# Attention rows with the maxima inside the query buffer, and the first expert layer joined to its normalisation

## The chip, the cores and the metric

The kernel runs on one core of a Trainium2 chip. The metric is the device time of one execution in microseconds. A profiled execution gives the trace; the other runs give times alone.

## What is computed

Two transformer layers with adaptive normalisation over 1024 tokens of width 256, in float32 with some bfloat16 in the expert part. Cut to what matters here:

```
layer 0: x -> modulated layer norm -> attention, 16 heads of 16, 1024 queries against 4096 keys
         scores = Q K^T / 4;  attn = softmax(scores);  out = attn V;  x += gate * (out Wo^T)
         x -> modulated layer norm -> router over 8 experts, top 2, softmax weights
         h = silu(x w1) * (x w3), bfloat16, 8 experts of 64 units;  x += gate * (weights, h w2)
layer 1: x -> modulated layer norm -> attention, 16 heads of 16, 1024 queries against 1024 keys, projection, bias
         x -> norms -> causal attention, 16 heads of 128 -> router over 16 experts, top 6
         -> experts of 176 units and a shared one of 352;  x += gate * result
```

## The kernel before, in words

All instructions are written out by hand for each engine, with semaphores between them; each `nc.Block()` ends in a barrier of all engines. The order within an engine is the order of the code.

**Narrow attention** (class `Attention`, `run`, used for both layers; `nkt` is 32 key tiles of 128 in layer 0 and 8 in layer 1). A unit `u` is one half (512 queries) of one head, 32 units per layer. Every unit has two passes. The *first pass* (`first_half`, L706) multiplies queries by keys so that VectorE can take the row maxima (L901 in layer 0, L896 in layer 1); a chunk is a pair of products, one on each *strip* of TensorE's rows (rows 0 to 63 and 64 to 127), which run side by side. The *second pass* (`second_chunk`, L770) computes the transposed scores minus the maximum, tile by tile on alternating strips, ScalarE takes the exponential (L1003) and the value products (`values_part`, L749) sum probabilities times values. Queries and keys are split in a high and a low part, 16 rows each, so a strip has 48 rows for the first pass and 51 for the second, the last three of which are the maximum in three parts against rows of ones in the keys. PSUM has four banks for the first pass, a ring of three (4 to 6) for the second, bank 7 for the values.

**The turn of the maxima.** The maximum of a query lies in a column; the second pass needs it as a row. GpSimd splits it in three bfloat16 parts (`split_max`, L624 to L630), written twice, for both strips, into a field of 115 columns that is zero elsewhere. `turn_maxima(u)` on TensorE (L722) first multiplies the query rows by an identity (L728, 112 rows to 115 rows, 512 columns), then adds four products that turn the parts (L733), so that one PSUM bank holds queries and maxima. ScalarE copies it to the buffer `q_max` (`put_row`, L952), which the second pass reads. The turn for unit `u + 1` stands ahead of `second_chunk(u, turn_at)`, with `turn_at = nkt - 6`, that is 26 in layer 0 and 2 in layer 1, and takes one place in the ring of three banks.

In `slot_long` (layer 0) the order on TensorE for four key tiles j to j + 3 is:

```
second(j)  first_pair(strips 1, 0)  second(j + 1)  values, half 0
second(j + 2)  second(j + 3)  first_pair(strips 0, 1)  values, half 1
```

`second(j)` is the turn if it is due, the wait for the bank (the exponential three places earlier in the ring), and the product. Even j are on strip 0, odd on strip 1. `slot_short` (layer 1) is `second(j)`, `first_pair(1, 0)`, `second(j + 1)`, the turn if due, `first_pair(0, 1)`, `second(j + 2)`, `second(j + 3)`, values.

SyncE issues nearly all transfers in one queue: it stores each unit's result (L152), loads the next head's query rows (`send_rows`, L73; three parts for each strip) into one of `nb` buffers `q_rows` (3 or 4), and its keys (L432) and values (L435). ScalarE issues six transfers at the start of layer 1 alone.

**The front** of layer 0 (`Front`, and the loop over `ahead` chunks in `run`) computes the modulation, the first norm and the query projection; `pick_queries` (L839) puts the first head's queries in place, and `half_product` (L1390) of the projection stands between the first chunks.

**After the first attention** come two blocks: `normalise` "n1" (L1284: statistics, square root on ScalarE at L1339, transposes L1332, the normalised, transposed tokens `h_t` at L1319 and L1346; SyncE loads the router's and the experts' weights in it, L1272) and `experts_low` (L1505: eight filling products, 32 router products L1584, ScalarE casts the weights at L1619 to L1624, VectorE ranks the experts L1473 to L1482 and then makes their weights L1493 to L1501; the up products L1557, SiLU L1609, `weigh` L1643 and L1647, transposes L1566, down products L1577). `experts_high` (L2225 on) uses the same `rank_experts` and `best_softmax`; there the first hidden product of VectorE (L2509) stands between the two. `keep_busy` (L1281) are products whose result nobody reads.

## Time and profile before

| | |
|---|---|
| median of 3 runs | 1763.31 us (1759.29 to 1764.13) |
| the profiled execution | 1766.98 us, its span in the trace 1765.1 us |
| TensorE busy | 1702.8 us, 96% of the span |
| VectorE, ScalarE, GpSimd busy | 1390.3, 1151.6 and 525.8 us |
| granted TensorE clock | 0.987 of full, mean |
| layer 0 attention | from about 53 to 736 us |
| norm and experts of layer 0 | 736 to 783 us |
| layer 1 narrow attention | 783 to 1024 us |
| wide attention, then the experts of layer 1 | to 1534, to the end |

A busy TensorE is not one at its peak, since ends of products are modelled; the starts are what the trace measures, so paces are read between starts. A row of the timeline merges equal instructions that follow each other: its second number is from the first one's start to the last one's end.

### The profile page before, as it was taken

What the parts mean: (1) busy time and instruction counts of PE and PEld (TensorE: products, weight loads), DVE (VectorE), ACT (ScalarE), POOL (GpSimd) and SP (SyncE); (2) the same over time, 40 slices, a digit from 0 to 9 for tenths busy, and PEclk for the clock granted to TensorE, in tenths of its full rate; (3) what the DMA queues carried; (4) which work ended last, traced back from release to release, by engine and by line L of the source; (5) the groups of instructions that cost most, each with busy time, mean ns of one, the idle gap of its engine ahead of it and who ended that gap; (6) DMA issues with size and microseconds to landing.
All of it is one profiled execution on the core that took longest, in us unless ns stands there. A gap on an engine that the chain in (4) does not pass through costs nothing. (4 is left out here: it accounts for less than half of the span.)

```text
span 1765.1 us, 33568 instructions
## 1 busy us (share of the span) xinstructions
PE 1702.8 (96%) x12503; PEld 1042.5 (59%) x12506; DVE 1390.3 (79%) x1930; ACT 1151.6 (65%) x2279; POOL 525.8 (30%) x549
## 2 busy tenths in 40 slices
PE   9999999999999999889999989999999999899998
PEld 6433333333333333565444468888888888778886
DVE  6999999999999996367999667677777777566665
ACT  3788888888888887555888545455545555543433
POOL 7646334334444512002334301110211120044221
PEclk8999999999999999989999999999999999999999
DMA  5223222223322300103546210000000000034332
GB/s 169 50 46 59 47 52 53 48 46 73 70 47 58 77 20 11 37 19 60 134 100 168 70 33 16 9 24 15 24 9 24 15 12 1 13 102 114 104 106 77
DMA packets 50329, 97.48 MB, mean 55 GB/s; under 512 B 11313, under 2 KB 21649, under 8 KB 48771
## 3 DMA queue, kind: packets, MB, share of 16 engines
q1 hardware_dynamic: 50019, 95.58, 22.5%
q8 instruction: 78, 1.28, 0.3%
q10 hardware_dynamic: 192, 0.30, 0.1%
q14 instruction: 40, 0.33, 0.1%
HBM read 64.58 MB, written 15.92 MB: 46 GB/s over the span
## 5 line engine op out<-in xcount | busy, mean ns | idle before, releaser
L1003 ACT ACTIVATE a_probs<-psum 128x512 f32<-128x512 f32 x1280 | 693.1, 597 | 122.5 <-PE psum L770 94.0
L901 DVE TENSOR_REDUCE a_max_part<-psum 128x1 f32<-128x1024 f32 x512 | 621.3, 1223 | 40.0 <-PE psum L706 37.1
L770 PE MATMUL psum<-a_q_max,a_k_rows 51*128 51x512 f32 x1280 | 409.5, 466 | 0.8 <-ACT a_probs L1003 0.7
L749 PE MATMUL psum<-a_probs,a_v_ext 128*32 128x256 f32 (+1 forms) x4600 | 395.2, 415 | 7.0 <-issue 6.9
L706 PE MATMUL psum<-a_k_rows,a_q_rows 48*128 48x512 f32 x1280 | 354.3, 428 | 1.1 <-ACT a_q_rows L969 0.7
L770 PEld LDWEIGHTS psum<-a_q_max,a_k_rows 51*128 51x128 f32 x1280 | 167.0, 184 | 270.0 <-ACT a_probs L1003 215.0
L749 PEld LDWEIGHTS psum<-a_probs,a_v_ext 128*32 128x32 f32 x4600 | 91.4, 108 | 207.1 <-ACT a_probs L1003 105.4
L706 PEld LDWEIGHTS psum<-a_k_rows,a_q_rows 48*128 48x128 f32 x1280 | 152.1, 186 | 17.0 <-DVE a_max_part L901 6.8
L896 DVE TENSOR_REDUCE a_neg_max<-psum 128x1 f32<-128x1024 f32 x128 | 150.8, 1219 | 8.4 <-PE psum L706 8.1
L2360 PE MATMUL psum<-high_t_parts,high_gu 128*128 128x512 f32 x600 | 148.0, 396 | 0.8 <-DVE high_hid L2509 0.8
L624 POOL TENSOR_TENSOR a_max_bf<-a_neg_max,a_zeros 128x8 bf16<-128x8 f32 x64 | 14.6, 228 | 431.1 <-issue 391.3
L461 POOL TENSOR_TENSOR a_k_rows<-a_k_in,a_k_rows 16x2048 fp32r<-16x2048 f32 x30 | 137.0, 4565 | 2.3
L1924 PE MATMUL psum<-wide_k_t,wide_q_t 128*128 128x512 f32 (+3 forms) x576 | 130.5, 353 | 1.5 <-DVE wide_k_t L2122 1.5
L2360 PEld LDWEIGHTS psum<-high_t_parts,high_gu 128*128 128x128 f32 x600 | 113.5, 190 | 27.9 <-POOL high_gu L2477 1.4
L1924 PE MATMUL psum<-wide_p_t,wide_v 128*128 128x512 f32 (+3 forms) x576 | 109.7, 344 | 5.1 <-DVE x L2133 5.1
L1924 PEld LDWEIGHTS psum<-wide_p_t,wide_v 128*128 128x128 f32 x576 | 97.6, 188 | 22.5 <-issue 6.3
L2065 ACT ACTIVATE wide_probs<-psum,wide_neg_max 128x128 f32<-128x128 f32 (+7 forms) x128 | 96.4, 753 | 21.6 <-DVE wide_neg_max L2155 21.6
L2144 DVE TENSOR_TENSOR wide_p_t<-psum,wide_p_t 128x512 fp32r<-128x512 f32 (+1 forms) x192 | 99.9, 548 | 12.4 <-ACT wide_p_t L2050 12.4
L1924 PE MATMUL psum<-wide_t_parts,wide_wqk 128*128 128x512 f32 x384 | 102.2, 401 | 6.1 <-DVE wide_v L2122 3.9
L2050 ACT ACTIVATE wide_p_t<-psum 128x512 fp32r<-128x512 f32 (+1 forms) x192 | 87.1, 493 | 28.1 <-PE psum L1965 28.1
L1924 PEld LDWEIGHTS psum<-wide_k_t,wide_q_t 128*128 128x128 f32 x576 | 94.0, 189 | 12.6 <-issue 1.9
L2155 DVE TENSOR_REDUCE wide_neg_max<-psum 128x1 f32<-128x128 f32 (+7 forms) x128 | 97.0, 758 | 4.4
(282 smaller groups left out, 2162.7 us busy)
## 6 DMA issues: line engine op xcount, KB each, us to landing
o<-a_o_out SPq DMA_DIRECT2D x56, 256.0 KB, 2.3
a_k_in<-in_k SPq DMA_DIRECT2D x90, 128.0 KB, 4.6
a_q_rows<-q_high SPq DMA_DIRECT2D x122, 64.0 KB, 2.4
gu_in<-in_w_gu SPq DMA_DIRECT2D x25, 256.0 KB, 2.9
high_cw<-cw SPq DMA_DIRECT2D x22, 256.0 KB, 4.0
a_v_in<-in_v SPq DMA_DIRECT2D x16, 256.0 KB, 5.8
a_o<-o SPq DMA_DIRECT2D x8, 512.0 KB, 4.2
wide_qk_in<-in_wqk SPq DMA_DIRECT2D x16, 256.0 KB, 2.7
```

The lines of the kernel that those rows point to most:

```text
L461: pool.tensor_tensor(self.k_rows[low, b, :], self.k_in[low, :], self.k_rows[low, b, :], ALU.subtract).then_inc(self.k_split, 1)
L706: return pe.matmul(psum[:, 2 * (n % 2) + s, :], q_rows[rows, b, q0:q0 + P], k_rows[rows, b, k0:k0 + 512], start=True, stop=True)
L749: mm = pe.matmul(psum[32 * g:32 * g + 32, 7, cols], self.v_ext[:, b, block_at, :], self.probs[:, j % self.pring, cols], start=(j < 4 and f ...
L770: pe.matmul(psum[:, self.bank_of(self.filling(j)), :], k_rows[rows, b, k0:k0 + P], self.q_max[rows, u % 2, :], start=True, stop=True).then ...
L896: dve.tensor_reduce(self.neg_max[:, u % 2, c:c + 1], psum[:, 2 * (n % 2):2 * (n % 2) + 2, :], AX.XY, ALU.max, negate=True).then_inc(self.s ...
L901: dve.tensor_reduce(self.max_part[:, u % 2, qt, ch:ch + 1], psum[:, 2 * (n % 2):2 * (n % 2) + 2, :], AX.XY, ALU.max).then_inc(self.s1_free, 1)
L1003: act.activation(self.probs[:, p % self.pring, :], psum[:, self.bank_of(self.filling(j)), :], ACT.Exp).then_inc(self.exp_done, 1)
L1924: mm = pe.matmul(out, left(a), right(b), start=(first and n == 0), stop=(last and n == len(PARTS) - 1))
L2065: act.activation(probs[:, i % 2, 0:(i + 1) * P], bank_pair(i)[:, 0:(i + 1) * P], ACT.Exp, bias=neg_max[:, i:i + 1], accum_out=den[:, h % 2 ...
L2144: dve.tensor_tensor(turned_of(i, bank, 1), turned_from(i, bank), turned_of(i, bank, 0), ALU.subtract).then_inc(pt_lo, 1)
L2155: dve.tensor_reduce(neg_max[:, i:i + 1], bank_pair(i)[:, 0:(i + 1) * P], AX.X, ALU.max, negate=True).then_inc(max_ready, 1)
L2360: mm = pe.matmul(psum[:, 2 * (k % 2) + i, :], gu[:, par, a, at:at + P], t_parts[:, b, c, half * 512:(half + 1) * 512], start=(c == 0 and n ...
```

## The change

The change has several parts.

1. A strip is now 64 rows for both passes: rows 0 to 15 of the keys are ones, and rows 0 to 2 of the queries hold the maximum's three parts; the query parts move to rows 16 to 63. The second pass reads `q_rows`; `q_max` and the product with the identity (L728) are gone. The turn is four products with three columns each, ScalarE copies three rows into the first strip (`put_row`), and one key tile later it issues a transfer of these rows into the second strip (`copy_row`), for which `second_chunk(u, 1)` waits (`row_copied`). When a buffer is loaded for a new head SyncE also sends zeros into the rows 0 to 2 of each strip, two transfers per head (`zero_maxima`). `turn_at` is 25 in layer 0; in layer 1 it stays 2.
2. The experts' weights of layer 0 are loaded at unit 6 of the first attention and cast by GpSimd at units 8 to 10 (class `LowWeights`). `normalise` becomes the class `Normal`, whose instructions share one block with `experts_low`; 20 and 8 filling products there are gone, and the router products begin with half of the tokens.
3. `rank_experts` computes maximum and difference ahead of the ranking instead of after it (both expert layers), and `experts_low` reorders ScalarE.
4. ScalarE loads the table of the square root at the end of both narrow attentions and of `experts_low`.
5. Fourteen filling products follow `pick_queries(0, 2)` in the front.

```
-        self.turn_at = nkt - 6
+        self.turn_at = nkt - (7 if nkt > 8 else 6)
...
+    def zero_maxima(self, sp, b):
+        sp.wait_ge(self.zeros_ready, 1)
+        zero = self.zeros[0:MROWS, 0:P].unsqueeze(1).broadcast_to([MROWS, TT, P])
+        for first in (0, STRIP):
+            sp.dma_start(self.q_rows[first:first + MROWS, b, :].bitcast(F32).rearrange("p (a n) -> p a n", n=P), zero).then_inc(self.q_loaded[b], 16)
...
                     load_q(sp, (0, 1), q_rows[:, got % nb, :], got, self.q_loaded[got % nb])
+                    if got >= nb:
+                        self.zero_maxima(sp, got % nb)
...
+                if low_weights is not None and u == 6:
+                    low_weights.load(sp, front)
+                if low_weights is not None and u == 16:
+                    low_weights.given_back(sp)
...
+                if low_weights is not None and u in (8, 9, 10):
+                    low_weights.round(pool, u - 8)
...
-                pe.matmul(psum[0:QMAX_ROWS, bank, :], self.ident_r[0:STRIP + MROW, 0:QMAX_ROWS],
-                          q_rows[0:STRIP + MROW, b, half * QH:(half + 1) * QH], start=True, stop=False)
                 pe.wait_ge(self.max_ready, u + 1)
                 for t in range(4):
-                    parts = self.max_bf[:, u % 2, t, :, :].rearrange("p s r -> p (s r)")
-                    mm = pe.matmul(psum[0:QMAX_ROWS, bank, t * P:(t + 1) * P], parts[:, 0:QMAX_ROWS], self.ident_bf[:, :], start=False, stop=(t == 3))
+                    mm = pe.matmul(psum[0:MROWS, bank, t * P:(t + 1) * P], self.max_bf[:, u % 2, t, :], self.ident_bf[:, :], start=True, stop=True)
...
                 if j == 0:
                     pe.wait_ge(self.row_ready, u + 1)
+                if j == 1:
+                    pe.wait_ge(self.row_copied, 16 * (u + 1))
...
-                          self.q_max[rows, u % 2, :], start=True, stop=True).then_inc(self.s2_full, 1)
+                          q_rows[rows, b, half * QH:(half + 1) * QH], start=True, stop=True).then_inc(self.s2_full, 1)
...
                 pick_queries(0, 2)
+                keep_busy(pe, psum, self.ident_bf, 14, 3)
...
+            def copy_row(u):
+                act.wait_ge(self.row_ready, u + 1)
+                act.dma_start(rows_of_maxima(u, STRIP).bitcast(F32), rows_of_maxima(u, 0).bitcast(F32)).then_inc(self.row_copied, 16)
...
                     if j == self.turn_at and u + 1 < us:
                         put_row(u + 1)
+                    if j == self.turn_at + 1 and u + 1 < us:
+                        copy_row(u + 1)
...
+            act.activation(self.one[:, :], self.zeros[:, 0:1], ACT.Sqrt).then_inc(self.table_loaded, 1)
...
+    def load(self, sp, front):
+        router, gate, up, down = self.drams
+        sp.wait_ge(front.later_taken, 8)
+        sp.dma_start(self.router[:, :, :], router).then_inc(self.loaded, 16)
+        sp.dma_start(self.up_in[:, 0, :, :], gate).then_inc(self.loaded, 16)
+        sp.dma_start(self.up_in[:, 1, :, :], up).then_inc(self.loaded, 16)
+        sp.dma_start(self.down_in, down).then_inc(self.loaded, 16)
+    def round(self, pool, n):
+        if n == 0:
+            pool.wait_ge(self.loaded, 64)
+        if n < 2:
+            pool.tensor_copy(self.up[:, n, :, :], self.up_in[:, n, :, :]).then_inc(self.cast, 1)
+        else:
+            pool.tensor_copy(self.down_bf[:, :, :], self.down_in).then_inc(self.cast, 1)
+            pool.wait_ge(self.cast, 3)
+            pool.tensor_copy(self.down[:, :, :], self.down_bf[:, :, :]).then_inc(self.wide, 1)
...
     step(dve.tensor_copy(s[:, :, :].rearrange("p t e -> p (t e)"), scores))
+    step(dve.tensor_reduce(best[:, :], s[:, :, :], AX.X, ALU.max))
+    dve.tensor_tensor(e[:, :, :], s[:, :, :], best[:, :].unsqueeze(2).broadcast_to([P, TT, n_exp]),
+                      ALU.subtract).then_inc(less_ready, 1)
...
-            keep_busy(pe, psum, ident_bf, 8)
             for t in range(TT):
+                if t % 4 == 0:
+                    normal.half_ready(pe, t // 4)
...
-            for i in range(2):
-                act.activation(w_bf[:, i, :, :], w_in[:, i, :, :], ACT.Copy).then_inc(w_ready, 1)
             act.wait_ge(one_set, 1)
             act.activation(one[:, 1:2], one[:, 0:1], ACT.Exp).then_inc(table_loaded, 1)
...
+            act.wait_ge(less_ready, 1)
+            act.activation(e[:, :, :], e[:, :, :], ACT.Exp).then_inc(exp_ready, 1)
             take_hidden(0)
+            silu(0)
             take_hidden(1)
-            silu(0)
             silu(1)
```

## Rows read from the trace of the kernel before

**Rows 1.** Window, length; busy PE, PEld, DVE, ACT, POOL; clock, DMA share, GB/s.

```profile
200.00:400.00 200.00, 197.52 (x1913) 75.32 (x1905) 189.50 (x166) 176.58 (x330) 74.68 (x61) 1.00 0.27 51
```

**Rows 2.** Timeline of PE around one turn, first attention: start, length, engine, line.

```profile
315.72 0.64 PE L749 MATMUL psum<-a_probs,a_v_ext 128*32 128x256 f32 x8
316.29 0.72 PE L706 MATMUL psum<-a_k_rows,a_q_rows 48*128 48x512 f32 x2
...
316.95 0.64 PE L749 MATMUL psum<-a_probs,a_v_ext 128*32 128x256 f32 x8
317.52 0.49 PE L728 MATMUL psum<-a_q_rows,a_ident_r 112*115 112x512 f32 x1
317.85 0.39 PE L733 MATMUL psum<-ident_bf,a_max_bf 128*115 128x128 bf16 x4
318.17 0.50 PE L770 MATMUL psum<-a_q_max,a_k_rows 51*128 51x512 f32 x2
```

**Rows 3.** Timeline of DVE, first attention: the end of two units' maxima.

```profile
314.63 0.17 DVE L907 TENSOR_REDUCE a_neg_max<-a_max_part 128x4 f32<-128x16 f32 x1
...
335.30 0.17 DVE L907 TENSOR_REDUCE a_neg_max<-a_max_part 128x4 f32<-128x16 f32 x1
```

**Rows 4.** Timeline of PE near the end of the first attention.

```profile
711.96 0.50 PE L770 MATMUL psum<-a_q_max,a_k_rows 51*128 51x512 f32 x1
712.39 0.70 PE L307 MATMUL psum<-a_w,h_t 128*128 128x256 f32 x2
```

**Rows 5.** DMAs of line L73, issue durations ns min/median/max, and landing of all.

```profile
L73 ACTq DMA_DIRECT2D a_q_rows<-q_high x2: 612/1048/1485, 796.1 to 797.7; - x2
...
DMA to landing us min/median/max: 1.9/2.3/7.5
```

**Rows 6.** Timeline of PE and ACT, layer 1 narrow attention.

```profile
837.30 0.49 PE L770 MATMUL psum<-a_q_max,a_k_rows 51*128 51x512 f32 x1
...
838.96 0.50 PE L770 MATMUL psum<-a_q_max,a_k_rows 51*128 51x512 f32 x2
...
842.99 0.49 PE L770 MATMUL psum<-a_q_max,a_k_rows 51*128 51x512 f32 x1
...
837.83 1.08 ACT L1003 ACTIVATE a_probs<-psum 128x512 f32<-128x512 f32 x2 [0.54 <-PE psum L770]
...
840.92 2.07 ACT L1003 ACTIVATE a_probs<-psum 128x512 f32<-128x512 f32 x4 [0.45 <-PE psum L770]
```

**Rows 7.** Timeline of all engines after the first attention.

```profile
736.19 1.28 ACT L1339 ACT_TABLE_LOAD   x1 [5.71 <-PEq L2599]
...
740.20 1.43 ACT L1346 ACTIVATE h_t<-psum,mod_col 128x512 f32<-128x512 f32 x2
...
745.48 6.94 PE L1584 MATMUL psum<-w_router,h_t 128*128 128x8 f32 x32
...
752.46 0.23 DVE L1473 COPY low_s<-psum 128x64 f32<-128x64 f32 x1 [6.46 <-PE psum L1584]
...
759.01 0.42 DVE L1643 TENSOR_TENSOR low_hid_bf<-low_act,low_x 128x512 bf16<-128x512 bf16 x1 [2.02 <-ACT low_act L1609]
```

**Rows 8.** Timeline of PE at the start of the experts of layer 1.

```profile
1539.14 3.70 PE L2392 MATMUL psum<-w_router,h_t 128*128 128x16 f32 x32
...
1550.75 2.97 PE L2360 MATMUL psum<-high_t_parts,high_gu 128*128 128x512 f32 x12 [0.78 <-DVE high_hid L2509]
```

**Rows 9.** Windows in the front and later, columns as in rows 1.

```profile
17.30:20.70 3.40, 2.65 (x9) 0.91 (x7) 1.76 (x3) 1.20 (x3) 3.17 (x4) 1.00 0.13 49
21.00:31.00 10.00, 10.00 (x16) 3.19 (x17) 5.30 (x5) 1.68 (x3) 7.01 (x7) 0.50 0.78 275
...
744.50:758.00 13.50, 13.09 (x70) 11.15 (x72) 5.30 (x27) 8.91 (x12) 0.00 (x0) 0.50 0.01 2
...
1543.20:1546.40 3.20, 3.20 (x9) 2.42 (x9) 3.20 (x24) 0.28 (x2) 0.00 (x0) 0.50 0.43 123
```

**Rows 10.** Timeline of PE in the front.

```profile
23.63 0.79 PE L706 MATMUL psum<-a_k_rows,a_q_rows 48*128 48x512 f32 x2
...
26.36 0.79 PE L706 MATMUL psum<-a_k_rows,a_q_rows 48*128 48x512 f32 x2
```

More of the change, by code:

```diff
@@ L430, in load_k @@
             at = STRIP * n
-            for row in range(0, MROW, HD):
+            for row in range(FIRST_ROW, STRIP, HD):
                 sp.dma_start(self.k_in[at + row:at + row + HD, :], part).then_inc(self.k_loaded, 16)
@@ L521, in _, with run @@
             self.clear(pool)
-    def run(self, block, load_q, load_kr, q_loads, merge, projection, stats, front=None, weights=None):
+    def run(self, block, load_q, load_kr, q_loads, merge, projection, stats, front=None, weights=None, low_weights=None):
         psum, nkt, nb, steps, groups, group, us = self.psum, self.nkt, self.nb, self.steps, self.groups, self.group, self.us
@@ L992, in _ @@
             put_row(0)
+            copy_row(0)
             for u in range(us):
@@ L1463, in low_parts, with rank_experts @@
                                      ALU.mult, ALU.subtract).then_inc(self.low_done, 1)
-def rank_experts(dve, scores, n_exp, s, above, rank, steps, done):
+def rank_experts(dve, scores, n_exp, s, above, rank, best, e, steps, done, less_ready):
     def step(ins):
@@ L1535, in experts_low @@
         block = r.block()
+        normal.register(block, psum, x, stats, ident, ident_bf, scale_col, bias_col, h_t, behind=0)
         def up_bank(t, i):
@@ L2600, in adaln_two_layers @@
                     front.register(block, attention, i["c"], i["wmod"], i["ident"], i["x"], i["ln_w"], ln_w[:, :], chunks(i["wq0"]))
-                    attention.run(block, load_q, None, 6, merge, projection, stats, front)
+                    attention.run(block, load_q, None, 6, merge, projection, stats, front, low_weights=low_weights)
         with ExitStack() as part:
             h_bf = part.enter_context(nc.sbuf_tensor("h_bf", [P, DC, T], BF16))
-            w_router = part.enter_context(nc.sbuf_tensor("w_router0", [P, DC, 8], F32))
-            w_up = part.enter_context(nc.sbuf_tensor("w_up", [P, 2, DC, 512], F32))
-            w_down = part.enter_context(nc.sbuf_tensor("w_down", [P, 4, D], F32))
-            normalise(nc, "n1", psum, x, stats, ident, ident_bf, mod_col[:, 6:8], mod_col[:, 4:6], h_t,
-                      loads=[(w_router[:, :, :], chunks(i["router0"])),
-                             (w_up[:, 0, :, :], chunks(i["w1"])), (w_up[:, 1, :, :], chunks(i["w3"])),
-                             (w_down[:, :, :], chunks(i["w2"]))])
-            experts_low(nc, psum, h_t, h_bf, w_router, w_up, w_down, ident, ident_bf, gates[:, 1, :], x, stats)
+            experts_low(nc, psum, h_t, h_bf, mod_col[:, 6:8], mod_col[:, 4:6], low_weights, ident, ident_bf, gates[:, 1, :], x, stats)
+        low_part.close()
         with ExitStack() as part:
@@ L2631, in adaln_two_layers @@
                     wqkv = front.enter_context(nc.sbuf_tensor("wqkv", [P, DC, 3, D], F32))
-                    normalise(nc, "n2", psum, x, stats, ident, ident_bf, mod_col[:, 10:12], mod_col[:, 8:10], h_t,
-                              loads=[(wqkv[:, :, :, :].rearrange("p c i n -> p c (i n)"), chunks(i["wqkv1"]))],
-                              xn=merge.o4[:, 0, 0:2, :].rearrange("p g t -> p (g t)").rearrange("p (t n) -> p t n", n=D))
+                    with ExitStack() as before:
+                        normal = Normal(Room(nc, before, "n2", CLEARED),
+                                        merge.o4[:, 0, 0:2, :].rearrange("p g t -> p (g t)").rearrange("p (t n) -> p t n", n=D))
+                        normal.register(normal.room.block(), psum, x, stats, ident, ident_bf, mod_col[:, 10:12], mod_col[:, 8:10], h_t,
+                                        loads=[(wqkv[:, :, :, :].rearrange("p c i n -> p c (i n)"), chunks(i["wqkv1"]))])
                     projection = Projection(attention.room, psum, h_t, wqkv, 3, (q_high, k_high), (q_low, k_low), v_sb)
```

176 lines of the change are left out of this document (98 added, 78 removed).

## The prediction

> **What bounds the kernel now.** I read the windows first. In the first attention TensorE is busy 197.5 of 200 us, VectorE 189.5, ScalarE 176.6 and GpSimd 74.7, at full clock [rows 1]; it is here that most of the run is spent. The timeline of TensorE then shows a fixed beat: from one block of value products to the next 1.23 us, of which 0.66 are the two rounds of strip products ahead of the values [rows 2]. The turn is the one block that breaks it: 0.33 us from the identity product to the first turning product and 0.32 from there to the next second-pass product, 0.65 in all [rows 2]. A unit lasts 20.67 us, from one end of its maxima to the next [rows 3]; sixteen beats are 19.7, the turn 0.65, and some 0.3 is the wait for the value bank once a unit. So TensorE sets the end of layer 0's attention, with VectorE 5% behind. In layer 1 the unit is 5.69 us [rows 6], and there the chain is another: the exponential starts 0.53 us after its product, the second one ends at 837.83 + 1.08 = 838.91, and the pair of products that needs its bank starts at 838.96, 0.05 later [rows 6]. After the first attention nothing is dense: the blocks wait for tables, loads and a slow clock [rows 7, 9].
>
> **The turn in layer 0.** L728 goes in all 64 units, worth 0.33 us each where nothing else changes. But the turn also moves from 26 to 25, and this place is worse. Ahead of 26 it stood between value products and a new pair, both edges of a switch that TensorE made anyway. Ahead of 25 it stands between the first pass's product on strip 0 and the second pass's on strip 1, which used to run side by side as the second round of the 0.66. Now that strip product runs alone, 0.33 at most until the turn (half of 0.66); the turn takes its 0.32; then L770 on strip 1 runs alone, and a lone one holds the next full-height product back for 0.43 [rows 4]. With the first round that is 0.33 + 0.33 + 0.32 + 0.43 = 1.41 us, where before stood 0.66 and, further on, 0.65: 0.10 **more** per unit, not 0.33 less. Thirty-one turns stand in the stream: +3.1 us. The other end is that the torn pair costs nothing and L728's 0.33 is saved: 31 x -0.33 = -10.2. I take +3.1, since each edge has a row of its own kind, and keep both. The turn at the front saves 0.3.
>
> The Trainium skill says the same from another side (TensorEngine Tiling (Array Packing), Tiling Modes): changing the tiling mode drains TensorE. By that rule alone a turn in the middle of strip work buys two more drains and no gain can be counted on; rows 2 and 4 show edges of 0.3 to 0.4 us that agree.
>
> **The turn in layer 1** stays at 2 and loses its 0.33. The product behind it waits for an exponential that no edit makes earlier (0.05 us margin above), so the start at 838.96 stays and the saving is nothing: 0. Its other bound, 31 x -0.33 = -10.2, is excluded by that wait unless the chain before it moves too.
>
> **The transfer.** Its issue holds ScalarE's queue. Rows of before show such issues on ScalarE at 0.61 to 1.49 us, for 16 rows instead of 3 [rows 5]; a shorter one isn't shown, so the ends are near 0 and 1.49, and I take 0.61 as the nearest. In layer 0 it waits until `put_row` has ended, 0.60 after its start; by then the next exponential is already issued, and the one after is due 0.53 after a product that comes about 1.4 us behind `put_row`'s start. 0.60 + 0.61 fits ahead of it: 0. In layer 1 the fourth exponential starts some 0.2 late, and the 0.45 us of idleness ahead of the next run of four [rows 6] takes that up: 0. If the cover is gone, each tenth beyond about 0.7 us costs a tenth per unit. Queued behind the issue are the exponentials, for which the ring of three banks and so TensorE waits. The landing (2.3 us median, 7.5 at most [rows 5]) has about 3.5 us in either layer before `second_chunk(u, 1)`: 0. The wait for `row_ready` has no cost, an exponential stands between.
>
> **SyncE and GpSimd.** Two zero transfers per head, 50 in all, some 0.6 us each at the price of [rows 5]: 1.2 us of a queue in the 41 us of two units in layer 0 and 11.4 in layer 1. Behind them wait keys, values and the next store; heads are loaded several units ahead, which hides it. Four weight loads at unit 6 likewise. GpSimd's casts, a few us at units 8 to 10, follow the turn's split and lie in 63% of idle time [rows 1]; without it the keys of a later head would be late. The split itself gets narrower: nothing.
>
> **Behind the first attention.** `h_t` is ready at 740.20 + 1.43 = 741.63, but the router products start at 745.48, since the block waits for its loads; they take 6.94 us at half clock, against 3.70 for as many at full clock in layer 1 [rows 7, 8]. In the joined block the first half starts near 740.6 (0.35 earlier than now, since the table load of 1.28 us at 736.19 is gone from the path and only the wait for the variance is left), the second at 741.3; with 3.70/2 = 1.85 behind it and the overlap, all end near 744.3. Scores are copied at 752.46 now, so -8.1. Behind the scores VectorE's first product was at 759.01, 6.5 us later, held by ScalarE's order. In the new order exponential, first hidden tile, table of 1.28 us and SiLU end about 5.4 us behind the scores if the up products run at half clock as I expect: -1.1 more. Together -9. Bounds: -5, if the clock falls already in the router products, and -11. After the router products of layer 1, dense but 16 columns wide, the clock did fall [rows 8, 9], so here I assume full clock through them and half behind them. The Trainium skill (TensorE: Matmul & The Clock Gate, What's actually happening) says that activity releases the throttle and a busy engine runs at 2.4 GHz; by that rule the up products would run at full clock and the gain be 1 us larger. The fall after 3.30 us of dense narrow products at 1543 [rows 8, 9] speaks against it, so I don't count that.
>
> **Tables and ranking.** The square roots of the second norm and of the wide attention each lose the part of a table load that sticks out, 0.35: -0.7. In `experts_high` 0.5 us of VectorE work moves ahead of the ranking, and TensorE already waits there for VectorE's first product, 0.78 us [rows 8]: +0.5.
>
> **The front.** TensorE was busy 2.65 of 3.4 us, then the clock fell to 1.2 GHz from 21 to 31 us [rows 9]. There a chunk came every 2.73 us [rows 10], all of it TensorE. Fourteen fillers lie in the pause of 0.75 us. If the clock holds, four chunks take some 1.4 us each, half: 4 x -1.35 = -5.4; loads of the modulation that come later may take some back, so -4. If not, 0. I take -4, at little better than even.
>
> **Sum**: +3.1 - 0.3 + 0 + 0 - 9 - 0.7 + 0.5 - 4 = -10.4 us. Against the profiled execution, 1766.98 (1.9 around its span of 1765.1), that is 1756.6; the median of the runs, 1763.3, is 3.7 lower, so 1753.
>
> **Rivals.**
> *The turn is saved after all.* L728's 0.33 goes and the place costs nothing: 13.3 us below the forecast, 1740. For it: the pair's two rounds are only as tight as modelled. Against: the lone product's 0.43 [rows 4]. 0.15.
> *The clock still falls in the front*: 1757. For it: the fall is seen once, and no row shows that a microsecond of fillers prevents it. 0.20.
> *The seam gives half*, since one of its new waits comes last or the clock falls early: 1758 to 1760. 0.11.
> *ScalarE's issue blocks the exponentials*: the slower side. SyncE and ScalarE issued together at 797 and ScalarE's issue grew to 1.49 us [rows 5]. In layer 1 SyncE issues most of the time. Were it 1.49 each time, the exponentials would be late by 0.57 us per unit in both layers, 62 x 0.57 = +35: 1788; in half of layer 1's units alone +9: 1762. It decides from about 0.75 us per issue in layer 0 and 0.9 in layer 1. The Trainium skill (Perfetto Trace Analysis, DMA Instruction — HWDGE (DVE, Sync)) states that the descriptor generator is locked for exclusive use while it is configured and generates; that is this rival's mechanism, and the one group of issues here agrees. Against: in layer 0 SyncE is idle around the turn. 0.12 for a result slower than before, about 1775 to 1788.
> *The removed product is not removed from the path*, that is no attention effect at all: 1750, within the forecast.
>
> **Numbers.** Forecast's case 0.42, own range 1748 to 1757. About 0.3% (5.3 us) is what a measurement can tell from no change. Faster by more, below 1758: forecast 0.42, saved turn 0.15, most of the fallen clock 0.16: 0.73. Within: 0.16. Slower: 0.11. The range reaches from 1740 to 1765.
>
> **What would show it.** L728 absent; the beat of 1.23 unchanged; a block of about 1.41 us once a unit and a unit of 20.77 us in layer 0, 5.69 in layer 1; issues of ScalarE at 0.6 us; router products from about 741 and VectorE's first product some 9 us earlier; clock at full from 21 to 31 us. I am wrong if the unit of layer 0 falls to 20.3, if ScalarE's issues are over 0.8 us with TensorE idle behind them, or if `second_chunk(u, 1)` waits for the landing.

## The result, and the profile after

The changed kernel takes 1768.89 us in the median of 8 runs (1762.54 to 1770.48), the kernel before, on the same chip beside it, 1762.08 (1759.29 to 1767.35). The ratio is 1.0034, with a 95% interval of 1.0017 to 1.0050: 6 to 7 us slower, where 1753 was forecast, and outside the range. The profiled execution took 1768.72 us. Two executions further down stand far off and are in no ratio: one of the kernel before beside e1 to e4 (2238.51 us) and one of e12 (3770.79 us).

I read where the time lies from the exponentials of the two narrow attentions, since ScalarE's first and last ones bound the stages. In the timeline of ScalarE of the changed kernel (start, length) these are the first and last of layer 0 and the first and last of layer 1:

```profile
47.80 1.30 ACT L1023 ACTIVATE a_probs<-psum 128x512 f32<-128x512 f32 x2 [2.70 <-PE psum L779]
...
731.99 0.60 ACT L1023 ACTIVATE a_probs<-psum 128x512 f32<-128x512 f32 x1 [1.75 <-PE psum L779]
...
814.24 1.30 ACT L1023 ACTIVATE a_probs<-psum 128x512 f32<-128x512 f32 x2 [2.72 <-PE psum L779]
...
1010.86 0.60 ACT L1023 ACTIVATE a_probs<-psum 128x512 f32<-128x512 f32 x1 [0.56 <-PE psum L779]
```

The start of one to the start of the next of these four, from each trace, in us (the second trace of the kernel before is experiment e8, the last line the best version, e11):

| trace | front | attention 0 | between | attention 1 | rest | span |
|---|---|---|---|---|---|---|
| before, first trace | 53.09 | 675.01 | 92.32 | 187.06 | 757.67 | 1765.1 |
| before, second trace | 53.01 | 674.29 | 90.87 | 187.25 | 756.24 | 1761.7 |
| after | 47.80 | 684.18 | 82.26 | 196.62 | 756.03 | 1766.9 |
| after - first trace | -5.3 | +9.2 | -10.1 | +9.6 | -1.6 | +1.8 |
| forecast | -4.3 | +3.1 | -9.35 | 0 | +0.15 | -10.4 |
| e11 | 47.12 | 669.06 | 82.56 | 187.22 | 756.88 | 1742.8 |

Front, seam and rest came as forecast or a little better than that against the first trace; against the second, seam and rest are -8.6 and -0.2, close to the forecast. The two attentions lost 18.7 us where 3.1 was forecast. The windows show no new bound in the steady stretch, as [rows 1], and no slow clock in the front, as [rows 9] had it; but the clock is at half in three new places, of which these are two (the first line is the steady stretch, the next two the front, the last two those places; columns as in rows 1):

```profile
200.00:400.00 200.00, 197.82 (x1890) 74.09 (x1888) 188.37 (x165) 175.84 (x328) 77.06 (x66) 1.00 0.29 58
17.30:20.70 3.40, 3.40 (x24) 1.83 (x23) 2.21 (x3) 1.70 (x3) 3.17 (x4) 1.00 0.15 55
21.00:31.00 10.00, 9.97 (x41) 4.75 (x40) 8.68 (x8) 4.25 (x7) 9.22 (x9) 1.00 0.76 260
591.60:598.40 6.80, 6.46 (x35) 2.32 (x37) 2.45 (x2) 3.37 (x6) 0.00 (x0) 0.50 0.16 47
861.30:864.70 3.40, 3.38 (x16) 1.02 (x16) 2.44 (x3) 0.81 (x3) 0.00 (x0) 0.50 0.61 102
```

The page's groups name two waits of TensorE that the kernel before had not (busy, mean ns of one, idle before, releasers):

```profile
L779 PE MATMUL psum<-a_q_rows,a_k_rows 64*128 64x512 f32 x1280 | 427.6, 471 | 4.4 <-DMA a_q_rows<-a_q_rows 3.3
L716 PE MATMUL psum<-a_k_rows,a_q_rows 64*128 64x512 f32 x1280 | 356.2, 430 | 2.8 <-DMA a_k_rows<-k_high 2.1
```

**The turn in layer 0**, which answers to [rows 2], in the timeline of TensorE:

```profile
312.19 0.50 PE L779 MATMUL psum<-a_q_rows,a_k_rows 64*128 64x512 f32 x1
312.19 0.73 PE L716 MATMUL psum<-a_k_rows,a_q_rows 64*128 64x512 f32 x2
312.85 0.39 PE L740 MATMUL psum<-ident_bf,a_max_bf 128*3 128x128 bf16 x4
313.17 0.49 PE L779 MATMUL psum<-a_q_rows,a_k_rows 64*128 64x512 f32 x1
313.59 0.64 PE L756 MATMUL psum<-a_probs,a_v_ext 128*32 128x256 f32 x8
314.16 0.50 PE L779 MATMUL psum<-a_q_rows,a_k_rows 64*128 64x512 f32 x2
```

The block from the first strip product to the values lasts 313.59 - 312.19 = 1.40 us, where 1.41 was worked out: 0.66 for two rounds, 0.32 for the turn, 0.42 for the lone product. An ordinary unit is 20.77 us between the same exponentials of two units, against 20.67.

**The one long unit of layer 0.** Unit 26 lasts 27.05 us, 6.3 more than the others. In the same timeline:

```profile
587.89 0.73 PE L716 MATMUL psum<-a_k_rows,a_q_rows 64*128 64x512 f32 x2
591.94 0.76 PE L779 MATMUL psum<-a_q_rows,a_k_rows 64*128 64x512 f32 x1 [3.33 <-DMA a_q_rows<-a_q_rows]
592.63 1.08 PE L756 MATMUL psum<-a_probs,a_v_ext 128*32 128x256 f32 x8
```

TensorE stands 3.33 us for the row transfer, and works at half clock for the next 6.8 us, which costs the other 3. ScalarE had issued that transfer at 583.92, in 0.68 us as ever. What stood before it is seen in SyncE's queue and in the DMA view of 577 to 592 us (share of the 16 engines that is busy, in tenths of 40 slices):

```profile
577.85 2.66 SPq L428 DMA_DIRECT2D a_k_in<-in_k  x6
580.55 0.42 SPq L431 DMA_DIRECT2D a_v_in<-in_v  x1
581.07 0.37 SPq L181 DMA_DIRECT2D a_den<-o  x1
581.54 2.44 SPq L188 DMA_DIRECT2D a_o<-o  x4
```

```profile
DMA  0000359699993998894999799999999899994000
```

Keys, values and the sums of heads 8 to 11, 2.1 MB in all, keep the engines nearly full until 591. ScalarE's transfers have a queue of their own in the DMA view, q10 (SyncE's is q1). From the issue at 583.9 to 590.4 the view has the first of these lines and no q10; from 590.4 to 591.0 it has the second (packets, MB, share of the 16 engines):

```profile
q1 hardware_dynamic: 591, 1.33, 103.6%
q10 hardware_dynamic: 6, 0.01, 5.7%
```

So the row's first packet started 6.6 us behind the issue, and TensorE's wait ended 8.0 us behind it, where the second strip's product is due after 4.3. From the issue to the start of the last packet it is 1.6 us in the median of the 64 transfers, 3.3 at most in the others, and 6.9 here.

**Layer 1.** These are the durations of its units 0 to 30, worked out from the trace as the time between the first exponentials of two units, in us:

```
5.93 5.71 5.70 5.70 5.70 5.70 5.71 9.63 5.71 5.70 5.70 6.35 5.69 5.71 5.70 6.20
5.70 5.70 5.71 5.70 5.70 8.63 6.15 5.70 5.70 5.70 5.71 5.70 6.53 6.82 8.50
```

The ordinary unit is as it was (5.70 us). Six units (7, 11, 15, 21, 22 and 28) carry nearly all of the 9.6 us; the first and the last two are long in the kernel before as well. SyncE's timeline ahead of the longest shows issue upon issue, with some 0.05 us between them, from 843.1 on:

```profile
851.95 1.62 SPq L484 DMA_DIRECT2D a_q_rows<-a_zeros  x2
...
856.77 0.85 SPq L71 DMA_DIRECT2D a_k_rows<-k_high  x1
857.66 0.58 SPq L157 DMA_DIRECT2D a_w_direct<-in_wproj  x1
858.30 0.41 SPq L150 DMA_DIRECT2D o<-a_o_out  x1
858.75 0.43 SPq L157 DMA_DIRECT2D a_w_direct<-in_wproj  x1
```

and the timelines of TensorE and VectorE show who waits for its end:

```profile
859.11 0.50 PE L716 MATMUL psum<-a_k_rows,a_q_rows 64*128 64x512 f32 x2 [1.68 <-DMA a_k_rows<-k_high]
...
861.32 1.94 PE L756 MATMUL psum<-a_probs,a_v_ext 128*32 128x512 f32 x8 [1.05 <-ACT a_probs L1023]
...
860.53 0.69 DVE L925 COPY a_o_out<-psum 128x512 f32<-128x512 f32 x1 [3.56 <-DMA o<-a_o_out]
```

The last key rows (issued until 857.62) hold the first pass at 859.11. The store at 858.30 lets VectorE copy the sums only at 860.53, and TensorE's values, put down to an exponential that had long ended, start 0.1 behind that copy's end at 861.22. In the list of waits (us in total, times, longest), VectorE's wait for its own store is 12.4 us in 8 times over layer 1; in the kernel before that wait isn't in the list:

```profile
DVE a_o_out L925 <- DMA o<-a_o_out: 12.4, 8, 3.6
```

**Between the attentions**, which answers to [rows 7], counted from the last exponential (728.10 before, 731.99 after):

```profile
743.72 1.43 ACT L1436 ACTIVATE h_t<-psum,mod_col 128x512 f32<-128x512 f32 x2
...
744.53 3.74 PE L1672 MATMUL psum<-low_router,h_t 128*128 128x8 f32 x32 [0.23 <-ACT h_t L1436]
...
748.31 0.23 DVE L1563 COPY low_s<-psum 128x64 f32<-128x64 f32 x1 [1.53 <-PE psum L1672]
...
752.68 0.42 DVE L1727 TENSOR_TENSOR low_hid_bf<-low_act,low_x 128x512 bf16<-128x512 bf16 x1
```

`h_t` comes 0.4 us earlier (12.10 to 11.73 us behind that exponential), the router's products start 4.8 earlier and take 3.74 us instead of 6.94, the scores are copied 8.0 earlier (forecast 8.1), VectorE's first product 10.2 (forecast 9.2).

### The profile page after: what moved, and what is told of

It reads as the page before. It is cut to its first block and busy times, and to the rows that moved or that the text cites. A ratio compares the mean times of both kernels' runs of the same rounds, so it can differ in the third digit from the quotient of the medians.

```text
span 1766.9 us, 33652 instructions
## 1 busy us (share of the span) xinstructions
PE 1697.1 (96%) x12425; PEld 1024.8 (58%) x12428; DVE 1388.5 (79%) x1929; ACT 1149.5 (65%) x2278; POOL 523.0 (30%) x553
## 5 line engine op out<-in xcount | busy, mean ns | idle before, releaser
L779 PE MATMUL psum<-a_q_rows,a_k_rows 64*128 64x512 f32 x1280 | 427.6, 471 | 4.4 <-DMA a_q_rows<-a_q_rows 3.3
L716 PE MATMUL psum<-a_k_rows,a_q_rows 64*128 64x512 f32 x1280 | 356.2, 430 | 2.8 <-DMA a_k_rows<-k_high 2.1
L779 PEld LDWEIGHTS psum<-a_q_rows,a_k_rows 64*128 64x128 f32 x1280 | 170.5, 185 | 296.1 <-ACT a_probs L1023 234.2
L716 PEld LDWEIGHTS psum<-a_k_rows,a_q_rows 64*128 64x128 f32 x1280 | 152.0, 186 | 18.8 <-issue 8.6
L906 DVE TENSOR_REDUCE a_neg_max<-psum 128x1 f32<-128x1024 f32 x128 | 150.4, 1218 | 8.2 <-PE psum L716 7.9
L632 POOL TENSOR_TENSOR a_max_bf<-a_neg_max,a_zeros 128x4 bf16<-128x4 f32 x64 | 13.2, 207 | 432.6 <-issue 379.9
```

Of the source, the lines that this page charges most:

```text
L716: return pe.matmul(psum[:, 2 * (n % 2) + s, :], q_rows[rows, b, q0:q0 + P], k_rows[rows, b, k0:k0 + 512], start=True, stop=True)
L779: pe.matmul(psum[:, self.bank_of(self.filling(j)), :], k_rows[rows, b, k0:k0 + P], q_rows[rows, b, half * QH:(half + 1) * QH], start=True, ...
L906: dve.tensor_reduce(self.neg_max[:, u % 2, c:c + 1], psum[:, 2 * (n % 2):2 * (n % 2) + 2, :], AX.XY, ALU.max, negate=True).then_inc(self.s ...
```

## The experiments

The theory I went in with: the turn cost what was forecast, and the rest of the loss is two queues, the DMA engines in unit 26 and SyncE's in layer 1. The rival: the row transfer and its issue on ScalarE are at fault in both. All edits are to the changed kernel unless said otherwise, and all are timed beside the kernel before.

**e1: the turn back at 26.**

```
-        self.turn_at = nkt - (7 if nkt > 8 else 6)
+        self.turn_at = nkt - 6
```

> The changed kernel with layer 0's turn put back from 25 to 26, nothing else. Its unit in layer 0 lasts 20.77 us in the trace of the changed kernel, 20.67 before. Theory A (the place tears a pair of strip products and eats what the removed identity product gave): the unit falls to 20.77 - 0.10 - 0.33 = 20.34 us, 31 x -0.43 = -13.3 us in all, near 1755 us; the row transfer then has 4.31 - 0.6 = 3.7 us from its issue to the product that needs its row, so a late landing may cost more often than the one time seen. Theory B (the place is neutral; the identity product ran beside other work, and the 0.10 comes from ScalarE's issue): the unit stays between 20.7 and 20.8 us and the time near 1768 us. Layer 1 is as in the changed kernel under both.

Measured: 1759.17 us, ratio 0.9990 (0.9978 to 1.0001). The unit of layer 0 is 20.46 us, 0.31 less than with the turn at 25 and 0.21 less than before: nearer to A, but 0.12 short of it. Unit 26 is 25.55 us long again, layer 1 still 196.2. The place of the turn is worth 31 x 0.31 = 9.6 us. Where the 0.12 went is in TensorE's and ScalarE's timelines:

```profile
309.33 0.64 PE L756 MATMUL psum<-a_probs,a_v_ext 128*32 128x256 f32 x8
309.78 0.39 PE L740 MATMUL psum<-ident_bf,a_max_bf 128*3 128x128 bf16 x4
310.10 0.73 PE L779 MATMUL psum<-a_q_rows,a_k_rows 64*128 64x512 f32 x2
310.44 0.63 PE L716 MATMUL psum<-a_k_rows,a_q_rows 64*128 64x512 f32 x2
311.00 0.64 PE L756 MATMUL psum<-a_probs,a_v_ext 128*32 128x256 f32 x8
```

The pair of second-pass products lasts 0.73 us instead of the 0.50 of [rows 2]: the second one waits for its bank, whose exponential, the last of a row of four from 307.96 with 2.32 us, ends at 310.28. With the identity product gone ScalarE is next in the chain. The unit's account closes with it: -0.33 for the identity product, -0.12 since the turn now starts 0.45 us behind the value products (309.33 to 309.78) where the identity product started 0.57 behind them [rows 2], +0.24 for this wait, -0.21 together.

**e2: the zero rows by GpSimd.**

```
-            sp.dma_start(self.q_rows[first:first + MROWS, b, :]..., zero).then_inc(self.q_loaded[b], 16)
+            pool.memset(self.q_rows[first:first + MROWS, b, :].bitcast(F32), 0.0).then_inc(self.rows_zeroed, 1)
```

(in `copy_v`, ahead of the copy, and TensorE waits for it)

> The changed kernel with the six rows per head zeroed by two GpSimd memsets instead of two transfers that SyncE issues. Theory A (in layer 1 SyncE's queue became too long: 150 us of issues in 197 us against 126 in 187, so loads of queries and keys and stores come late and stop TensorE and VectorE): every unit of layer 1 is back at 5.70 us but for the last ones, the stretch from the first to the last exponential of layer 1 falls from 196.6 to about 188 us, and the time by 8 us to about 1761 us. Theory B (the late units of layer 1 come from the row transfer, its landing or its issue on ScalarE, or from contention between transfers): the units of 6.2 to 9.6 us stay, the time stays within 2 us of the changed kernel's. Layer 0 keeps its unit of 20.77 us in both.

Measured: 1773.47 us, ratio 1.0068 (1.0051 to 1.0085). The times fit neither. The trace does: the late units of 9.63, 8.63, 6.2 to 6.5 us are gone, and in their place every second unit is 6.55, all alike. GpSimd's timeline gives the reason:

```profile
855.56 1.94 POOL L483 MEMSET a_q_rows<- 3x1024 f32 x2 [4.56 <-DVE a_o_out L924]
857.58 0.46 POOL L479 TENSOR_TENSOR a_v_ext<-v_sb,a_zeros 128x128 f32<-128x128 f32 x1
858.00 0.21 POOL L629 TENSOR_TENSOR a_max_bf<-a_neg_max,a_zeros 128x4 bf16<-128x4 f32 x1
```

Two memsets on three partitions take 1.94 us and put off the split of the maxima, for which the turn waits 1.24 us. SyncE's issues in layer 1 fell from 150 to 128 us, and the irregular stops went with them; the edit brought a cost of its own, which e6 removes. It shows in layer 0 too, where units 4, 8 and 24 are 0.7 to 1.1 us longer than the others, and unit 26 is 24.27 us.

**e3: the second strip's row by a second ScalarE copy**, no transfer; the turning products write rows 0 to 2 and 64 to 66.

```
+                act.activation(rows_of_maxima(u, STRIP), psum[STRIP:STRIP + MROWS, ...], ACT.Copy).then_inc(self.row_copied, 1)
-                act.dma_start(rows_of_maxima(u, STRIP)..., rows_of_maxima(u, 0)...).then_inc(self.row_copied, 16)
```

> The changed kernel with the row for the second strip written by a second ScalarE copy out of PSUM (the turning products write rows 0 to 2 and 64 to 66) instead of a transfer; the zero transfers stay. ScalarE pays 0.57 us per unit instead of an issue of 0.68. Theory A: the single stop of 3.3 us in layer 0 and the slow clock behind it go (-6 us), the units of layer 0 stay at 20.77 us, since the turn still stands at 25; layer 1 keeps most of its late units (8 us), since SyncE's queue is as long as it was: about 1762 us. Theory B (the row transfer makes layer 1 late): layer 1's units are back at 5.70 us and the time falls by 14 us to about 1755 us.

Measured: 1772.99 us, ratio 1.0067 (1.0047 to 1.0088). Unit 26 is like its neighbours, as both said. But the units are 21.16 and 5.76 us, and the time is 11 us over A's: in layer 0 a copy of 0.59 us costs 0.39 per unit where an issue of 0.68 cost nothing. ScalarE's timeline has the two copies one behind the other:

```profile
318.36 0.59 ACT L965 ACTIVATE a_q_rows<-psum 3x512 fp32r<-3x512 f32 x1
318.97 0.59 ACT L966 ACTIVATE a_q_rows<-psum 3x512 fp32r<-3x512 f32 x1
319.58 1.57 ACT L1020 ACTIVATE a_probs<-psum 128x512 f32<-128x512 f32 x3
```

In layer 1 late units are left (6.92, 6.55, 6.41, 6.06, 5.96), against B, which wanted none, but they add up to 3.1 us and not to the 8 of A: with every zero transfer still in SyncE's queue, two thirds of the 9.4 us went with the row transfers. SyncE's issues take 145.5 us there against 150.4, and each unit is 0.06 longer, which gives its queue more time; which of these did it isn't separated. I had priced the copy and the issue as the same kind of time, and they aren't (e10).

**e4: all of the change but the rows of the maxima** (the kernel before with fillers, joined block, early weights, tables and ranking).

> The kernel before with only what the change does outside the rows of the maxima: fillers in the front, the joined norm and expert block with its weights loaded early, the square-root tables, the order of the ranking. Theory A (these gave 5.3 us in the front, 10.1 between the attentions and 1.6 behind the second, as the two traces show): 1762.1 - 17.0 = 1745 us, units of 20.67 and 5.69 us with no late one. Theory B (the early weight loads on SyncE or the casts on GpSimd disturb the attention, or the clock held in the front falls later instead): above 1750 us, with a longer unit near units 6 to 10 or a clock at half inside the first attention.

Measured: 1750.12 us, ratio 0.9942 (0.9924 to 0.9960). Units of 20.65 and 5.70 us, none late, no slow clock inside either attention: A on the mechanism; the time is 5 us over A's and just at B's bound. The gain against the median of the kernel before is 10.6 us and not 17, since the 17 were read against a profiled execution of 1766.98 us, 6.3 above that median (e8).

**e5: e1, and one load of sums per unit.**

```
-                    merge.load_sums(sp, 8, 12, range(4))
+                if 24 <= u < 28:
+                    merge.load_sums(sp, 8, 12, (u - 24,))
```

> The changed kernel with layer 0's turn at 26 (as in e1) and the four loads of 256 KB with the sums of heads 8 to 11, which SyncE issued together behind unit 24, issued one per unit behind units 24 to 27. Theory A (the row transfer of unit 26 was issued 0.4 to 2.3 us behind these loads and those of keys and values and stood behind them in the DMA engines; TensorE waited 3.3 us for it and the clock fell for 6.8 us): unit 26 of layer 0 falls from 25.55 us to 20.46 us, no stop over 0.7 us of TensorE is left in layer 0, the time is 5 us under e1's 1759.2, so about 1754 us. Theory B (a late landing that has to do with this unit but not with these loads, or a clock that falls for another reason): a unit of 24 to 27 us stays and the time stays near 1759 us. Layer 1 stays at about 196 us from its first to its last exponential under both.

Measured: 1752.88 us, ratio 0.9959 (0.9940 to 0.9978); 6.3 under e1. Unit 26 is 20.47 us, and its row's first packet starts 1.5 us behind the issue (577.43 to 578.93) and not 6.6. A: 0.8 MB less ahead of a 6 KB transfer, and its wait is gone.

**e6: e5, and the zero rows by GpSimd in the odd rounds**, away from the split that VectorE waits for.

```
+                if u % 2 == 1 and nb <= h < H:
+                    self.zero_maxima(pool, h % nb)
```

> As e5, and the rows are zeroed by GpSimd in the odd rounds, where nothing follows that VectorE waits for, not right ahead of the copy of the values as in e2. Theory A (e2's even loss of 0.85 us in every second unit of layer 1 came from two memsets of 0.94 us between two splits of the maxima, which held VectorE's buffer; and with SyncE's queue back at 128 us of issues nothing else is late in layer 1): units of 5.70 us throughout, 187 us from layer 1's first to its last exponential, 9 us under e5: about 1745 us, and 5 us under e4, by a unit of 20.46 against 20.65 us in layer 0. Theory B (memsets of GpSimd slow VectorE or the row transfers themselves make layer 1 late, wherever they stand): units over 6 us stay in layer 1 and the time is over 1750 us.

Measured: 1747.45 us, ratio 0.9917 (0.9888 to 0.9945). All units of layer 1 are 5.69 us but for the first and the last two, which are longer in every trace, and its attention takes 187.0 us instead of e5's 195.1. A: without the 24 zero transfers of 0.78 us in SyncE's queue nothing of layer 1's loss is left, row transfers and all; e3 took two thirds of it away from the other side. The loss is thus one of both kinds of transfer together, and either edit alone doesn't say whose it was. The span gives 4.0 of the 8.1 us; the stretch between the attentions was 2.2 longer and the rest 1.7 longer than in e5's trace, and no edit reached either. What differs there is the clock. The stretch between the attentions in e5's trace and in e6's (columns as in rows 1) is

```profile
716.82:798.84 82.02, 73.55 (x507) 51.29 (x508) 55.76 (x134) 41.36 (x76) 9.83 (x19) 0.94 0.17 33
717.01:801.20 84.19, 75.59 (x507) 53.65 (x510) 55.83 (x134) 41.37 (x75) 9.82 (x19) 0.92 0.17 31
```

with 10.2 us at half clock in the first and 13.7 in the second.

**e7: e4 without the fillers.**

```
-                keep_busy(pe, psum, self.ident_bf, 14, 3)
```

> As e4 (the kernel before with everything of the change but the rows of the maxima), without the 14 fillers in the front. Theory A (the fillers hold the clock at full from 21 to 31 us and give 4.6 us): the clock is at half for about 10 us in the front, the first exponential of layer 0 starts near 53.1 us instead of 48.5, the time is 4 to 5 us above e4's 1750.1, so about 1755 us. Theory B (the fall of the clock in the front was a chance of the one profiled execution of the kernel before): the first exponential starts before 50 us and the time stays within 1.5 us of e4's.

Measured: 1748.64 us, ratio 0.9931 (0.9905 to 0.9957), not slower than e4. The first exponential starts at 47.90. The numbers are B's; whether B's reason holds is seen in e8. The pause is there again and the clock doesn't fall:

```profile
17.30:20.70 3.40, 2.65 (x10) 0.91 (x8) 1.79 (x3) 1.43 (x3) 3.17 (x4) 1.00 0.14 54
21.00:31.00 10.00, 9.97 (x39) 4.54 (x39) 8.67 (x8) 4.32 (x8) 9.22 (x9) 1.00 0.74 259
```

The first line is that of [rows 9] almost to the digit, the second isn't. The order of TensorE's work is the same there as before; all of it lies 0.56 us earlier.

**e8: the kernel before again**, unchanged.

> The kernel before itself, unchanged, for a second trace. Its profiled execution took 1766.98 us, where its runs have medians of 1760.7 to 1763.3. Theory A (a part of the 16 us by which e4's trace is shorter was particular to that one execution): the new trace is some 3 to 6 us shorter than 1766.98 us, and the places where it differs (front, seam, or behind the second attention) say which term of the prediction was read too high; units of 20.65 to 20.67 and 5.69 us as before. Theory B (an execution under the profiler is simply that much longer for this kernel): 1766 to 1768 us again, with the same places.

Measured: a profiled execution of 1763.48 us, span 1761.7, 3.4 us under the first. A: the difference is 0.7 in layer 0, 1.5 between the attentions and 1.4 behind the second. The fall of the clock in the front is in both traces, which speaks against B of e7 (a chance of one execution), too. The 1.5 and 1.4 us come with the clock: 20.5 us at half between the attentions in the first trace and 13.7 in the second, 13.8 and 10.5 behind them.

**e9: the kernel before with the fillers alone.**

> The kernel before with the 14 fillers in the front and nothing else. In both traces of the kernel before the clock is at half for 10.2 us from 20.8 us, and the first exponential of layer 0 starts at 53.0 to 53.1 us; without fillers but with the rest of the change (e7) it does not fall, and the exponential starts at 47.9. Theory A (either is enough: what decides is how the pause of 0.75 us at 19 us lies to what the throttle looks at, and the fillers fill that pause): no fall in the front, the first exponential at 48 to 48.7 us, the time 4.5 us under the kernel before, about 1756 us. Theory B (the fillers do nothing; the fall is decided by the start of the kernel being 0.5 us earlier): the fall stays, the first exponential starts at 53 us, and the time is within 1 us of the kernel before.

Measured: 1758.83 us, ratio 0.9986 (0.9977 to 0.9996). The first exponential starts at 47.92, 5.1 us earlier: A on the mechanism. So the fillers hold the clock in this kernel, and the rest of the change holds it without them (e7). Of the 5.1 us only 2.3 reach the median; in the trace layer 1 is 1.3 and the rest 2.4 longer than in e8, and nothing was edited there. There too the clock was at half for longer, for 3.4 us in layer 1 (995.6 to 999.1; none in e8) and for 20.0 in the rest (10.5 in e8). The mean granted clock of its ten executions is 0.989 to 0.993, as is that of the fifteen of the kernel before beside them, so what the fillers hold in the front doesn't show in the means; why isn't settled.

**e10: e6 with a second issue on ScalarE.**

```
+                act.dma_start(self.row_scratch[0:MROWS, u % 2, :], rows_of_maxima(u, 0)...).then_inc(self.row_copied, 16)
```

> As e6, and ScalarE issues a second transfer of the same row, into a scratch tile, right behind the first, so that its queue is held for 1.37 us per unit instead of 0.68. Theory A (one issue has cover in both layers, as the prediction had it, up to 0.75 us in layer 0 and 0.9 in layer 1; beyond that each tenth costs a tenth): units of 20.47 + 0.6 = about 21.1 us in layer 0 and 5.69 + 0.45 = about 6.15 us in layer 1, 31 x (0.6 + 0.45) = +33 us, about 1780 us. Theory B (there is no such edge: the exponentials catch up behind it in one or both layers): units of 20.5 to 20.7 and 5.69 to 5.8 us, the time under 1757 us.

(TensorE waits for both transfers.)

Measured: 1781.19 us, ratio 1.0107 (1.0091 to 1.0122). Units of 21.16 and 6.12 us, 0.69 and 0.43 longer. A, in size too. ScalarE's timeline shows what covers one issue and not two:

```profile
319.31 0.57 ACT L1027 ACTIVATE a_probs<-psum 128x512 f32<-128x512 f32 x1
319.44 0.71 ACTq L973 DMA_DIRECT2D a_q_rows<-a_q_rows  x1
320.18 0.68 ACTq L974 DMA_DIRECT2D a_row_scratch<-a_q_rows  x1
320.91 0.60 ACT L1027 ACTIVATE a_probs<-psum 128x512 f32<-128x512 f32 x1 [1.03 <-PE psum L782]
```

The queue issues while the engine still computes the exponential that was handed to it before. The second copy of e3 has ScalarE to itself for its 0.59 us.

**e11 and e12: the best version.** e11 is e6 without the fillers. e12 is the same, with SyncE's zero transfers in layer 0 alone.

> As e6, without the 14 fillers in the front, which e7 showed to hold nothing in that order of work. Theory A: the clock stays at full in the front without them, the first exponential is 0.1 to 0.6 us earlier, the time equal to e6's 1747.4 or up to 1.5 us under it. Theory B (the front of this kernel is another than e7's, and the clock falls without fillers): the first exponential starts near 52 us, and the time is 4 to 5 us over e6's.

> As e11, but in layer 0 the rows are zeroed by the two transfers per head that SyncE issues, as in the change; in layer 1 by GpSimd. Theory A (in layer 0 SyncE has 41 us per head and the zero transfers cost nothing; all of their cost lay in layer 1): units of 20.47 and 5.69 us, the time within 1.5 us of e11's, perhaps under it, since units 4, 8 and 26 of layer 0, which were 0.2 to 0.4 us long in e6, lose that. Theory B (they delay keys and values in layer 0 too): late units in layer 0, the time 3 us or more over e11's.

Measured: e11 1744.74 us, ratio 0.9904 (0.9889 to 0.9919); e12 1744.61, ratio 0.9903 (0.9887 to 0.9918). A for both. Without fillers the first exponential starts at 47.12 instead of 47.58. Units of 20.46 and 5.70 us in e11; in e12 20.47 and 5.69. The zero transfers cost nothing in layer 0 beyond 0.3 us over the whole attention; of the units that were to lose their excess only unit 8 did (units 4 and 26 are 20.83 and 21.05). Either is 16 us under the kernel before and, since the change is 6.8 above it, some 23 under the change.

## Why the prediction was wrong

- **The turn in layer 0** was right: +3.1 forecast, a block of 1.40 us against 1.41, a unit of 20.77 us to the digit. The bound of -10.2 (the product's full 0.33 saved) isn't reached even at the good place: e1 gives 0.21, since the exponential ends some 0.2 us too late for the second product of the pair.
- **The turn in layer 1**: right, 5.70 us before and after.
- **The issue on ScalarE**: right. 0.68 us against 0.61, no cost. In e10 the two issues take 1.42 us and cost 0.69 and 0.43; counted one for one that puts the edges at 0.73 and 0.99 us, where the text had 0.75 and 0.9. By its own edges the rival's issue of 1.49 would have cost 0.74 in layer 0 and not the 0.57 that it took for both layers. The rival that had the slower side to itself was wrong about the place: its 0.12 covered only one queue of three.
- **"The landing has about 3.5 us ... : 0" failed.** In layer 0 the issue was 4.3 us ahead of the product that needs the row, enough in all units but one, where the row came 8 us behind it. The row that gave 2.3 us median and 7.5 at most [rows 5] was in hand; the maximum was set aside for the median, and nobody asked what stands ahead of the transfer in each unit. It cost 6.3 us, half of it by the clock. It is also the one of the text's own signs of being wrong that came: `second_chunk(u, 1)` waited for the landing. The Trainium skill (DMA: Bandwidth & Descriptors, Issuing engines are not separate DMA queues) says that transfers of all issuing engines run on the same 16 DMA engines and interleave; the trace agrees that they share them, and shows no interleaving for 6.6 us: so long the row's first packet stood, while the other queue moved 591.
- **"SyncE ... a queue in ... 11.4 in layer 1" failed, and it is the largest miss: 9.6 us against 0.** The text took 1.2 us per head and measured 1.6 (0.75 to 0.83 us each), but the size isn't the point. e6 shows that it was these transfers, and e3 that it took the row transfers beside them. The text compared the addition with the length of two units and not with what the queue already held: 126 of 187 us on the mean, and full, without gap, in the stretches in which SyncE also loads the weights of the merge. "Heads are loaded several units ahead" was never read from a row. The lead is finite, and the stores behind the loads have none. The Trainium skill (Perfetto Trace Analysis, What "DMA-bound" means) lists an issuing queue that is solid with slices as one of the things that can bind; the rows from 851.95 on are such a queue.
- **The seam and the tables**: right, -10.1 against -9.35, or -8.6 against the second trace. The router's products ran at full clock, 3.74 us against the 3.70 taken (the text has 3.30 for them in one place). The clock fell to half at 748.64, right behind them, as the text had it. VectorE's first product all the same stood 4.4 us behind the scores (748.31 to 752.68) and not 5.4, which is the excess.
- **The front**: right in size (-5.3 against -4.3), and by luck as to the cause. The fillers do it in the kernel before (e9), but the changed one, with its later edits, holds the clock without them (e11). What decides is open: the same pause, 0.56 us earlier, didn't bring the clock down. e7 and e9 show only that either edit is enough.
- **The sum**: against the first trace the misses are +6.1 in layer 0, +9.6 in layer 1, -1.0, -0.7 and -1.8 elsewhere, 12.2 together: 1756.6 forecast for the profiled execution, 1768.7 found. In the medians the miss is 17.2 us, +6.8 for -10.4. The other 5 are the step from the profiled execution to the median: it is -4.9 for the kernel before (1766.98 to 1762.08; the text took -3.7 for both) and nothing for the one after (1768.72 to 1768.89). The first trace of the kernel before was long by its clock (e8), and savings read from it are read too high.

## What to carry to other kernels

Price a new transfer in three places: the queue that issues it, the queue's other load in the fullest stretch and not on the mean, and what is on the DMA engines when it is issued; for a transfer with a deadline in every unit, look at each unit. An issue on ScalarE's queue hid here under the exponential that ran already, a copy of nearly the same length didn't. Look for the product that tears a pair of strips before moving anything between them.

## What the runs showed that was not expected

- Behind one and the same pause of 0.75 us in the front the clock falls to half in both traces of the kernel before and not in e7, with the same order of products on TensorE, 0.56 us earlier.
- A GpSimd memset of 3 x 1024 elements takes 0.94 us on the mean of 50 in e2 (1.94 for the two shown), more than the issue of the transfer that it replaces (0.78 us). One of 128 x 1024 takes 0.94 too, in the same trace: few partitions saved nothing.
- One late product of 3.33 us costs almost as much again by the clock behind it: 27.05 - 20.77 - 3.33 = 2.95 us.
- Stretches that no edit touches differ by some 2 us from trace to trace, and the clock goes with it. Between the attentions the joined kernels have 10.2 us at half clock and last 82.0 to 82.6 us (after, e3, e5, e7, e10, e11), or 13.7 and 83.7 to 84.2 (e1, e2, e4, e6, e12); none lies between. What decides which of the two comes is open. Single terms below 2 us are therefore read from units, not from totals.
